# Graph attention kernel: norms of row pairs 1 to 3 moved from the opening into the step loop

## What is computed

```python
def gat(item, ent, adj, W, a):
    s = (item @ W @ a[:64, 0])[:, None] + (ent @ W @ a[64:, 0])[None, :]
    e = jnp.where(s > 0, s, 0.2 * s)
    e = jnp.where(adj > 0, e, -9e15)
    return elu(softmax(e, axis=1) @ ent + item)
h = relu(layernorm(x))                 # the norm that is moved by the change
x = x + gat(h, ent, adj, W, a)
h = relu(layernorm(x))
x = x + (adj == 1).astype(f32) @ h + h
```

## Time and profile before

| | us |
|---|---|
| median of the runs | 421.19 |
| profiled execution | 419.45 |
| its span | 417.6 |
| TensorE matmul busy | 370.3 |
| VectorE busy | 318.8 |
| ScalarE busy | 194.5 |
| GpSimd busy | 133.3 |

### The profile page before, as it was taken

How to read it: one execution, slowest core, us unless ns; L and a number is a source line. 1 busy time by engine, 2 the same in 40 slices (tenths; PEclk the granted TensorE clock), 3 DMA queues, 4 the chain that set the end, 5 groups by cost and what they waited for, 6 DMA issues and landing times. The chain is left out here.

```text
span 417.6 us, 5471 instructions
## 1 busy us (share of the span) xinstructions
PE 370.3 (89%) x2181; PEld 133.0 (32%) x2181; DVE 318.8 (76%) x382; ACT 194.5 (47%) x247; POOL 133.3 (32%) x190
## 2 busy tenths in 40 slices
PE   1795898898987689899979999998789999999896
PEld 1562522222321113233312233323222433334464
DVE  2653768999799998988979787999797899844211
ACT  1400345565645556654456556534465564642100
POOL 7698410111312217621112151045070737000500
PEclk9979599999999999999999999999999999999999
DMA  8999999676635999999998999955569999999511
GB/s 274 213 213 214 213 213 212 116 123 100 102 56 97 154 157 149 167 119 157 182 152 126 148 141 132 136 50 52 50 54 106 108 107 107 105 108 107 61 52 50
DMA packets 25385, 54.14 MB, mean 130 GB/s; under 512 B 1872, under 2 KB 10128, under 8 KB 25104
## 3 DMA queue, kind: packets, MB, share of 16 engines
q0 software_dynamic: 24192, 50.34, 85.6%
q1 hardware_dynamic: 1008, 3.42, 2.2%
q10 hardware_dynamic: 160, 0.03, 0.0%
HBM read 136.63 MB, written 1.05 MB: 330 GB/s over the span
## 5 line engine op out<-in xcount | busy, mean ns | idle before, releaser
L584 ACT ACTIVATE yp<-yp,tbias 128x1024 f32<-128x1024 f32 (+1 forms) x160 | 154.3, 977 | 127.3 <-DVE yp L804 126.0
L804 DVE SCALAR_TENSOR_TENSOR yp<-s8b,t8neg,am 128x1024 f32<-128x1024 f32 (+1 forms) x160 | 168.1, 1076 | 24.7 <-PE pb L1081 16.2
L1068 PE MATMUL pb<-yp,enta 128*64 128x512 f32 x384 | 102.5, 616 | 16.7 <-ACT yp L584 16.6
L359 POOL DMA_DIRECT2D am<-adj_t x64 | 35.3, 557 | 144.5 <-DVE yp L804 144.5
L717 DVE TENSOR_TENSOR am<-am,vx 128x2048 uint16<-128x2048 uint16 x64 | 79.5, 1243 | 0.7 <-ACT vx L505 0.7
L1062 PE MATMUL pb<-yp,enta 128*65 128x512 f32 x128 | 64.0, 619 | 7.6 <-ACT yp L584 7.5
L1081 PE MATMUL pb<-yp,onesf 128*32 128x512 f32 x384 | 51.1, 605 | 0.0
L1068 PEld LDWEIGHTS pb<-yp,enta 128*64 128x64 f32 x384 | 21.3, 136 | 69.3 <-ACT yp L584 42.0
L991 PE MATMUL pb<-edge,h 128*64 128x512 fp8e4 x288 | 39.9, 384 | 0.0
L1062 PEld LDWEIGHTS pb<-yp,enta 128*65 128x65 f32 x128 | 15.1, 139 | 41.8 <-ACT yp L584 25.0
L991 PEld LDWEIGHTS pb<-edge,h 128*64 128x64 bf16 x288 | 17.0, 111 | 34.5 <-issue 29.8
(11 more groups left out here) (156 smaller groups left out, 314.1 us busy)
## 6 DMA issues: line engine op xcount, KB each, us to landing
am<-adj_t POOLq DMA_DIRECT2D x76, 512.0 KB, 10.2
edge<-adj_t POOLq DMA_DIRECT2D x12, 512.0 KB, 9.3
edge<-adj_t POOLq DMA_DIRECT2D x8, 256.0 KB, 7.2
am<-adj_t POOLq DMA_DIRECT2D x8, 256.0 KB, 22.2
enta<-ent SPq DMA_DIRECT2D x1, 1040.0 KB, 5.0
xs<-xt SPq DMA_DIRECT2D x1, 1024.0 KB, 8.1
out<-yp SPq DMA_DIRECT2D x4, 256.0 KB, 2.0
mats<-eye SPq DMA_DIRECT2D x1, 256.0 KB, 5.4
```

The lines of the kernel that those rows point to most:

```text
L359: pool.dma_start(am[:, q % RING], adj_t[q]).then_inc(landed[q % RING], 16)
L584: sc.activation(y, y, ACT.Exp, bias=tbias[:, jt:jt + 1]).then_inc(exp_done, 1)
L804: v.scalar_tensor_tensor(out=yp[:, n % YS, 0:W], in0=s8b[:, b % 2, 0:W], scalar=t8neg[:, jt:jt + 1], in1=am[:, (chunk0[b] + c) % RING, jt ...
L1068: t.matmul(acc2(b)[s * D:(s + 1) * D, :], enta[:, jt, 0:D], yp[:, n % YS, s * HALF:(s + 1) * HALF], start=(jt == 0), stop=(jt == NT - 1), ...
```

## The change

Pair 0's norm alone stays ahead of step 0. Those of pairs 1 to 3 start at steps 3, 34 and 50 (`NORM_AT`): centring, squares and relu there, the variance two steps later, `spread_out` three steps later in GpSimd's list, `deviation` at +8, `normed` at +12, `s_cols` at +14. All use one PSUM bank (`pb[:, 3]`) in turn, and `part` in place of `yp` as scratch. The load of `xs` becomes two, pair 0 apart, and the two small loads of W and a move from ScalarE's queue to the head of SP's. GpSimd issues chunks 8 to 22 in a row after pair 0's diagonals. On TensorE the variance of pair 0 goes behind the transpose of the limits.

```diff
     LONE_AT = 6
+    NORM_AT = {1: 3, 2: 34, 3: 50}
...
         ld_x = sem("ld_x")
+        ld_xs = sem("ld_xs")
         landed = [sem(f"landed{k}") for k in range(RING)]
...
         def _(sp):
+            sp.dma_start(wt_sb[:], w_t).then_inc(ld_w, 16)
+            sp.dma_start(a_sb[:], a_cols).then_inc(ld_w, 16)
             sp.dma_start(enta[:], ent).then_inc(ld_ent, 16)
             sp.dma_start(mats[:], eye).then_inc(ld_eye, 16)
-            sp.dma_start(xs[:], xt).then_inc(ld_x, 16)
+            sp.dma_start(xs[:, 0], xt[:, 0]).then_inc(ld_x, 16)
+            sp.dma_start(xs[:, 1:NP], xt[:, 1:NP]).then_inc(ld_xs, 16)
             for p in range(NP):
...
                 link(g.tensor_tensor(rstd0[:, p], rstd0[:, p], mhalf[:], ALU.pow))
-                g.tensor_tensor(yp[:, p].rearrange("p (t k) -> p t k", k=P),
+                g.tensor_tensor(part[:, 0:2].rearrange("p h (t k) -> p (h t) k", k=P),
                                 eyef.unsqueeze(1).to_broadcast([P, 2 * SUB, P]),
...
                 load(q)
-            for p in range(NP):
-                spread_out(p)
-                for q in range(8 + 2 * p, 10 + 2 * p):
-                    load(q)
+            spread_out(0)
+            for q in range(8, RING):
+                load(q)
...
-            q, v = 16, 0
+            q, v = RING, 0
             for n in range(STEPS_ALL):
                 b, jt = n // NT, n % NT
-                while q < NC and (q < RING or step_past(q - RING) <= n):
+                while q < NC and step_past(q - RING) <= n:
                     load(q)
                     q += 1
+                for p, at in NORM_AT.items():
+                    if n == at + 3:
+                        spread_out(p)
                 while v < len(ORDER) and edges_at(v) <= n:
...
-            act.dma_start(wt_sb[:], w_t).then_inc(ld_w, 16)
-            act.dma_start(a_sb[:], a_cols).then_inc(ld_w, 16)
             act.wait_ge(wrow_ps, 1)
...
-            for p in range(NP):
+            def norm_squares(p):
                 act.wait_ge(x0_ps, p + 1)
-                sc.activation(yp[:, p, 0:HALF], pb[:, p], ACT.Square).then_inc(x0_sq, 1)
-                sc.activation(h0[:, p], pb[:, p], ACT.Relu).then_inc(x0_relu, 1)
+                sc.activation(part[:, 2], pb[:, 3], ACT.Square).then_inc(x0_sq, 1)
+                sc.activation(h0[:, p], pb[:, 3], ACT.Relu).then_inc(x0_relu, 1)
+            def norm_variances(p):
                 act.wait_ge(var0_ps, p + 1)
                 sc.copy(rstd0[:, p].rearrange("p (s c) -> p c s", s=2),
-                        rowp[:, p * 2 * SUB:(p + 1) * 2 * SUB].rearrange("p (c s) -> p c s", s=2)
-                        ).then_inc(var0_sb, 1)
-            def s_cols(pairs, src):
-                sc.copy(s8c[:, pairs.start * 2 * SUB:pairs.stop * 2 * SUB].rearrange("p (u s c) -> p u c s", s=2, c=SUB),
-                        src.rearrange("p (u c s) -> p u c s", c=SUB, s=2)).then_inc(s_col, 1)
+                        pb[:, 3, 0:2 * SUB].rearrange("p (c s) -> p c s", s=2)).then_inc(var0_sb, 1)
+            def s_cols(p):
+                act.wait_ge(s8c_ps, p + 1)
+                sc.copy(s8c[:, p * 2 * SUB:(p + 1) * 2 * SUB].rearrange("p (s c) -> p c s", s=2),
+                        pb[:, 3, 0:2 * SUB].rearrange("p (c s) -> p c s", s=2)).then_inc(s_col, 1)
+            norm_squares(0)
+            norm_variances(0)
             act.wait_ge(esum_ps, 1)
...
             s_rows(0, 0)
-            act.wait_ge(s8c_ps, 1)
-            s_cols(slice(0, 1), pb[:, 0, 0:2 * SUB])
+            s_cols(0)
             v_rows(0, 0)
...
                 sc.activation(y, y, ACT.Exp, bias=tbias[:, jt:jt + 1]).then_inc(exp_done, 1)
-                if n == 3:
-                    act.wait_ge(s8c_ps, 2)
-                    s_cols(slice(1, NP), pb[:, 3, 0:(NP - 1) * 2 * SUB])
+                for p, at in NORM_AT.items():
+                    if n == at:
+                        norm_squares(p)
+                    if n == at + 2:
+                        norm_variances(p)
+                    if n == at + 14:
+                        s_cols(p)
                 if b >= 1:
...
                 dve.wait_ge(x0_relu, p + 1)
-                v.tensor_tensor(h0[:, p], h0[:, p], pb[:, p], ALU.mult).then_inc(h0_ready, 1)
+                v.tensor_tensor(h0[:, p], h0[:, p], pb[:, 3], ALU.mult).then_inc(h0_ready, 1)
...
                 dve.wait_ge(um_ready, first[b + 1])
-                dve.wait_ge(s_col, 1 if b <= 1 else 2)
+                dve.wait_ge(s_col, pair(b) + 1)
                 v.tensor_scalar(vq[:, 3, 0:s], um[:, 0:s], STEPS / 2.0, -3e38, ALU.is_ge, ALU.mult)
...
             normed(0)
-            normed(1)
-            normed(2)
             dve.wait_ge(eyeb_ready, 1)
...
             shifts(0)
-            normed(3)
             put_shift(0, 0)
...
                     put_shift(b, c + 1)
+                for p, at in NORM_AT.items():
+                    if n == at + 12:
+                        normed(p)
                 if b >= 1:
...
+            def first_centred(p):
+                if p >= 1:
+                    pe.wait_ge(s_col, p)
+                pe.wait_ge(ld_x if p == 0 else ld_xs, 16)
+                t.matmul(pb[:, 3], centre, xs[:, p], start=True, stop=True).then_inc(x0_ps, 1)
             def variance(p):
                 pe.wait_ge(x0_sq, p + 1)
-                if p >= 1:
-                    pe.wait_ge(var0_sb, p)
+                pe.wait_ge(x0_relu, p + 1)
                 for c in range(SUB):
-                    at = (p * SUB + c) * 2
-                    mm = t.matmul(rowp[:, at:at + 2], yp[:, p, c * P:(c + 1) * P], mean2, start=True, stop=True)
+                    mm = t.matmul(pb[:, 3, 2 * c:2 * c + 2], part[:, 2, c * P:(c + 1) * P], mean2, start=True, stop=True)
                 mm.then_inc(var0_ps, 1)
...
                 pe.wait_ge(sd_ready, p + 1)
-                pe.wait_ge(x0_relu, p + 1)
                 for s in range(2):
-                    mm = t.matmul(pb[s * D:(s + 1) * D, p], onesf[:, 0:D], yp[:, p, s * HALF:(s + 1) * HALF],
-                                  start=True, stop=True, tile_position=(0, s * D))
+                    mm = t.matmul(pb[s * D:(s + 1) * D, 3], onesf[:, 0:D], part[:, s], start=True, stop=True,
+                                  tile_position=(0, s * D))
                 mm.then_inc(rstd0_ps, 1)
...
                 pe.wait_ge(w8_ready, 2)
-                if b == 0:
-                    pe.wait_ge(var0_sb, NP)
                 if b >= 1:
...
-            def s_cols(pairs, dst):
-                for k, p in enumerate(pairs):
-                    for c in range(SUB):
-                        at = (k * SUB + c) * 2
-                        mm = t.matmul(dst[:, at:at + 2], h0[:, p, c * P:(c + 1) * P], w8s[:], start=True, stop=True)
+            def s_cols(p):
+                pe.wait_ge(h0_ready, p + 1)
+                for c in range(SUB):
+                    mm = t.matmul(pb[:, 3, 2 * c:2 * c + 2], h0[:, p, c * P:(c + 1) * P], w8s[:], start=True, stop=True)
                 mm.then_inc(s8c_ps, 1)
...
                     if v == 0:
-                        pe.wait_ge(s_col, 2)
+                        pe.wait_ge(s_col, NP)
                     elif v - 1 in VISITS:
...
             pe.wait_ge(ld_eye, 16)
-            pe.wait_ge(ld_x, 16)
-            for p in range(NP):
-                t.matmul(pb[:, p], centre, xs[:, p], start=True, stop=True).then_inc(x0_ps, 1)
-            variance(0)
+            first_centred(0)
             pe.wait_ge(wrow_sb, 1)
...
             t.transpose(turned[0:2, 2 * P:3 * P], m2[:, 0:2], eyef).then_inc(m2t_ps, 1)
+            variance(0)
             pe.wait_ge(d2_ready, 1)
...
             t.matmul(turned[:, 3 * P:3 * P + 2], onesf[0:2, :], d2[:], start=True, stop=True).then_inc(lim_ps, 1)
-            for p in range(1, NP):
-                variance(p)
             pe.wait_ge(ld_ent, 16)
...
             pe.wait_ge(gtab_ready, 1)
-            for k in range(3):
+            for k in range(4):
                 biggest(0, k)
-            deviation(1)
             s_rows(0, 0)
-            pe.wait_ge(h0_ready, 1)
-            s_cols((0,), pb[:, 0])
-            biggest(0, 3)
-            biggest(0, 4)
-            deviation(2)
-            biggest(0, 5)
-            biggest(0, 6)
-            deviation(3)
-            biggest(0, 7)
+            s_cols(0)
+            for k in range(4, NQ):
+                biggest(0, k)
             turn(0, 0)
             v_rows(0, 0)
-            pe.wait_ge(h0_ready, NP)
-            s_cols(range(1, NP), pb[:, 3])
             for n in range(STEPS_ALL):
...
                         variance_again(b - 1)
+                for p, at in NORM_AT.items():
+                    if n == at:
+                        first_centred(p)
+                    if n == at + 2:
+                        variance(p)
+                    if n == at + 8:
+                        deviation(p)
```

(2 more changed lines are left out.)

## The result

The changed kernel takes 423.49 us (median of 13 runs, 421.52 to 426.71) against 421.36 for the kernel before (13 runs): ratio 1.0067, 95% interval 1.0044 to 1.0089. It is slower, where 420.7 and a small gain were forecast. Its profiled execution took 423.38 us with a span of 421.6.

The account below looks back on a forecast made before the run. It took the span as a head held by GpSimd's norms plus 160 steps bound alternately by TensorE and VectorE. Terms: 7.5 - 2.9 - 0.7 - 2.1 - 1.3 = 0.5 us faster, 420.7 us by the median, range 416.2 to 425.0.

Parts of the forecast that it names:

- The head: Opening up to the first y: norms leave it, chunk 7's landing binds; sums at 30.0, first y 7.5 us earlier (6.8 to 8.5).
- I take 0.7: In the head: the two small loads ahead of enta on SP's queue move the loads by 0 to 1.1 us, taken as 0.7.
- Steps 0 to 13: TensorE bound: 3.1 us of pair 1's work, 0.5 gap, 0.9 for the clock; 4.6 us of gain remain (2.8 to 6.3).
- Steps 14 to 31: VectorE bound: normed(1) adds 0.69 us, the other additions lie in slack; 3.9 us of gain remain.
- Pair 2: Steps 32 to 49: TensorE's work costs 1.1 us and GpSimd's diagonals 1.0, sum 2.1; 1.8 us of gain remain.
- The port: GpSimd's diagonals delaying a VectorE instruction in pairs 2 and 3: taken as 1.0 us, between 0.13 and 1.6.
- Pair 3: Steps 50 to 63: TensorE's part almost free, VectorE gets 0.69 + 1.0, of which 1.3 us stay; 0.5 us remain.
- the dearer end of the range: The port's upper value: 1.6 us of delay on VectorE for each of pairs 2 and 3, 1.2 more in all.
- the power beside L804: Row cited on VectorE beside GpSimd's power: L804 still takes 1.28 us, so it doesn't show the skill's exclusion rule.
- Slower: Rival: diagonals come late in pairs 1 and 2, TensorE stands still 1 to 1.5 us each; 424.1 us, chance 0.27.
- Mostly kept: Rival: TensorE's additions in pairs 2 and 3 fill idle time, port costs 0.13; 2.8 us kept, 418.4 us, chance 0.33.
- the change doesn't do what it says: Rival: GpSimd's 15 loads in a row fill the queue, or chunk 7 lands much later; 424.4 us, chance 0.06.

Follow-up runs that it names:

- queues alone: The kernel before with only the two small loads of W and a moved to the head of SP's queue, xs in one load: 422.78 us, 1.0037.
- split alone: The changed kernel with the loads of W and a back on ScalarE's queue, xs still in two loads: 421.10 us, 1.0013 to the kernel before.
- the loads put back: The changed kernel with all opening loads as before (W and a on ScalarE's queue, xs in one load): 421.09 us, 0.9986 to the kernel before.
- ScalarE's copies: All loads as before, ScalarE making the diagonals of pairs 1 to 3 by eight small copies; pair 3 from step 50: 419.81 us, 52: 418.66, 58: 422.32.
- without the wide operation: The changed kernel with GpSimd's 128x1024 diagonals of pairs 1 to 3 replaced by a two-column copy: 420.18 us, 0.9995 to the kernel before.
- the variance done twice: All loads as before, steps as in the change, TensorE's eight small variance matmuls of pair 3 done twice: 419.92 us, 0.9982.
- the eight pieces: All loads as before, steps as in the change, GpSimd's wide diagonals operation cut into eight of 128x128: 423.30 us, 1.0053.
- step 52 instead of 50: All loads as before, GpSimd's wide operation as in the change, pair 3's norm from step 52: 417.96 us, 0.9930; with ScalarE's diagonals 418.66 us, 0.9953.

## Where the prediction was right and where not

**The head: right in its mechanism, 2.6 us too good.** The first step that failed is "I take 0.7" for the loads. It priced the later issue by the delay of the issues, 0 to 1.1 us, and the split at nothing. Both delayed the chunks, by 1.0 (queues alone, in the kernel before) and 1.4 (split alone: chunk 7 at 30.2 against 28.8), together 3.0. What fits all four is the bytes that missed the fast first microseconds, not the time of the issue. The page of before had it: 274 GB/s in its first slice, 213 in the next. With the loads put back the head came out at 29.9 and 38.1, the numbers of the sum, but that is partly luck: the sum holds the 0.7 for later loads, which that kernel doesn't have. Without it it would be 29.3, and the ten heads with these loads lie at 29.4 to 30.0.

**Steps 0 to 13: 2.9 forecast, 0.9 paid.** The work came as counted (centring 1.02, variance 0.95, deviation 1.08), but the clock rose sooner than assumed. The table by stage of the changed kernel gives 0.81 where before had 0.51:
```profile
40.00:54.00 14.00, 11.02 (x44) 3.35 (x44) 10.21 (x15) 6.80 (x12) 2.04 (x3) 0.81 1.06 214
```
TensorE was still at 1.2 GHz for 2.9 us after its first step, not 7, below the lower bound of 3.4, for which no row stood. The kernel before had 5.0 us of the low level after its first step, so by estimate (2.1 us less at half speed) the clock gave about 1 us back instead of costing 0.9. And 0.9 is the low end: in the eleven kernels with pair 1's diagonals by GpSimd (or none) this stretch loses 0.9 to 1.9 us, in step with the time at the low level after the first step (2.8 us for 0.9, 4.0 for 1.5, 5.2 for 1.9, the level read from the granted clock in windows of a quarter us). The three with ScalarE's copies lie 0.4 above that line. What sets the time of the rise no run shows.

**Steps 14 to 31: 0.7 forecast, 0.6 paid.** Right.

**Pair 2: 2.1 forecast, 1.4 paid.** The port was taken at 1.0; it cost 1.0 (1.4 against 0.4 without the wide operation). TensorE's part was nearly hidden (0.4 in all without the port's share), 1.1 had been kept for it.

**Pair 3: 1.3 forecast, 3.5 paid.** This is the second step that failed, and two of its sentences were wrong. "TensorE has 3.5 us idle here and takes its part almost free" reads a sum over the stretch as if it were free everywhere: in the first five steps TensorE has a fixed appointment, the turn of block 2's maxima, and what stands ahead of it is paid in full (0.9 for 0.95 of added matmuls, with the variance done twice). And the port's 1.0, of which 0.4 was to fall into VectorE's waits, was 1.4 with nothing to fall into, because VectorE's waits lay before it and after it. With `normed` (0.69) this makes up the 3.5: about 1.4 port, 1.4 wait for the turn, 0.7.

**The sign.** At y 64 the forecast was +0.5 and -1.5 was measured: 2.6 too little from the head and 2.2 from pair 3, against 2.0 and 0.7 too much feared for steps 0 to 13 and pair 2. Either of the two failed steps was enough. With the loads alone put back, y 64 comes at +0.5, the number of the forecast, but only because the errors in the steps cancel.

On the exclusion the trace agrees with the rule of the Trainium skill ("SBUF — State Buffer", the part on the engine side of the ports) as far as the wide operation goes: a y of 2.17 instead of 0.74, an L767 of 2.08 instead of 0.69, a `put_shift` of 2.92 instead of 1.22, each time 0.1 to 0.2 us less than the length of GpSimd's operation (1.9, beside the `put_shift` 2.36) less what had already run. So the dearer end of the range was the right value, 1.4 to 1.7 each, and the nearest row was that of the same GpSimd instruction (L656, 1.6). But the rule alone would have missed that pair 1's stretch cost nothing, since TensorE was behind.

The prediction took the power beside L804 (y still 1.28) for a row against the exclusion. It was read from the wrong side: that y started first, at 160.84, and it was GpSimd's power, begun at 161.06, that took 2.59 us instead of 1.67. Who starts first keeps its length in these rows. A y that started 0.36 us into a power was not held (timeline of the kernel before), though a y that started into the wide operation was; so the power is no stand-in for the wide operation:
```profile
108.57 1.66 POOL L440 TENSOR_TENSOR rstd<-rstd,mhalf 128x8 f32<-128x8 f32 x1
...
108.93 0.75 DVE L804 SCALAR_TENSOR_TENSOR yp<-s8b,t8neg,am 128x512 f32<-128x512 f32 x1 [0.50 <-PE pb L1062]
```

**The rivals.** "Slower" came, but not by its mechanism: `deviation` never waited for GpSimd in the changed kernel. A round took 3.9 to 4.7 us and not the 6 of the estimate, and pair 1's six steps lie in the slower steps 5 to 11, 9.0 us from its variance to its `deviation`, not the 6.5 taken from steps 16 to 31. Only the eight pieces brought this wait about. "Mostly kept" had TensorE and VectorE overlap; they did for pair 2, not for pair 3. That the change doesn't do what it says: GpSimd's 15 issues in a row took 8.05 us and held nothing up.

**Behind step 64.** The prediction had nothing there; the profiled execution lost another 0.8 us to step 70 and 1.7 after step 159, in stretches of low clock, as the tables by stage show (changed, then before):
```profile
141.00:156.00 15.00, 12.98 (x58) 2.54 (x58) 14.03 (x16) 9.16 (x10) 3.83 (x6) 0.78 1.12 165
...
396.00:422.00 26.00, 22.44 (x192) 14.01 (x188) 3.06 (x5) 0.00 (x0) 1.52 (x4) 0.91 0.11 41
```
```profile
141.00:156.00 15.00, 12.38 (x64) 2.64 (x60) 14.77 (x17) 8.87 (x10) 3.14 (x6) 1.00 1.12 172
...
396.00:422.00 26.00, 18.48 (x172) 11.77 (x168) 2.77 (x4) 0.00 (x0) 0.00 (x0) 0.99 0.11 41
```
Both stand near a pause of TensorE (block 2's first steps, and the wait of 2.07 us for the last h), but the kernel before has the same pauses and kept its clock in its profiled execution, so the pause alone doesn't explain them. Of the fifteen changed or edited kernels seven were profiled with such a stretch between 393 and 405 us; these seven lose 1.7 us after step 159 and the others nothing. They are not in every run: by the mean granted clock, the changed kernel's runs fall at 421.5 to 421.8 us (0.975), 422.8 to 423.8 (0.959 to 0.968) and 425.9 to 426.7 (0.955 to 0.959), the runs of before at 419.3 to 421.3 (0.971) and 421.0 to 422.5 (0.967). The best group against the best is about 1.5 us, the loss at step 64; the rest of the 2.1 in the medians goes with the clock. The two groups of before are 1.7 us apart, so it too seems to meet one such stretch in about half of its runs, though not in the profiled one. Whether the change makes the low stretches more frequent, or only meets them otherwise, no run here settles.

## What to carry to other kernels

A stage's idle sum says how much work it can take, not where: look for the next instruction in the stage that another engine waits for, and put the moved work behind it. When two such placements are compared, take a point behind all of the moved work: measured at block 2's first y, step 52 instead of 50 looked like 1 us, and by y 96 it was 0.4. Here a GpSimd product of 1.9 us cost the VectorE instruction that started behind it 1.4 to 1.7 us, and its stretch 1.0 to 1.4 where VectorE was full and nothing where TensorE was behind. Handing it to ScalarE gained 1.4 us for pair 3 from step 50, and 0.1 or a loss at every other place tried; cut into eight it took 6.79 us beside pair 2 and TensorE waited for it. And the order of bulk loads in the first microseconds is part of the critical path as soon as the head is bound by a load: two small loads ahead of the first large one, or a large one cut in two, cost 1.0 and 1.4 us, and both together 3.0.

## What the runs showed of the hardware that was not expected

Two small loads (32 KB and 0.5 KB) ahead of a large one, on the same queue, moved its issue by 1.24 us and a whole stream of later loads by 1.0; one load cut in two (256 and 768 KB, same bytes) moved that stream by another 1.4 to 2.0. GpSimd and VectorE held each other off, and the profile shows it as a longer instruction and not as a wait: a product of 1024 columns and 1.90 us stretched the VectorE instruction behind it by 1.4 to 1.7, eight products of 128 columns doubled most VectorE instructions of 8 columns beside them (0.16 to 0.32), a y that had started first stretched a power of 8 columns from 1.67 to 2.59, and a y that started into a power of 1.66 kept its 0.75. And executions of one and the same program differed by 5 us in 423, in step with TensorE's mean granted clock (0.975 to 0.955).
